# Moving the quantise parts on VectorE from ahead of the factors to ahead of the accumulation

## What is computed

```python
def _L0_attn_ref(hidden_states, w_q, w_k, w_v, w_o):
    q, k, v = ((hidden_states @ w).reshape(B, S, H, Dh) for w in (w_q, w_k, w_v))
    scores = einsum('bqhd,bkhd->bhqk', q, k) * scaling + mask
    attn = softmax(scores, axis=-1)
    return einsum('bhqk,bkhd->bqhd', attn, v).reshape(B, S, H * Dh) @ w_o

def fp4_quant_dequant(x):                     # blocks of 16 along the last dim
    scale = max(max(abs(xb)) / 6.0, 1e-12)
    idx = searchsorted(_MID, abs(xb / scale))
    return _GRID[idx] * sign(xb) * scale

def fp4_linear(x, w):
    return einsum('bsk,nk->bsn', fp4_quant_dequant(x), fp4_quant_dequant(w))
```

## Time and profile before

| | us |
|---|---|
| median of 3 runs | 483.98 |
| lowest to highest | 483.85 to 485.07 |
| the profiled execution | 483.85 |
| its span (first to last instruction) | 482.0 |

### The profile page before, as it was taken

One profiled execution on the slowest core, in us unless ns is written; L12 is line 12 of the kernel. 1 busy time (PEld: TensorE's weight loads), 2 busy tenths in 40 slices (PEclk: granted clock), 3 DMA queues, 4 the chain that ended last, 5 costly groups with the idle time before them and its releaser, 6 DMA issues.

```text
span 482.0 us, 17248 instructions
## 1 busy us (share of the span) xinstructions
PE 442.8 (92%) x6418; PEld 347.0 (72%) x6418; DVE 404.4 (84%) x1368; ACT 331.6 (69%) x972; POOL 298.1 (62%) x501
## 2 busy tenths in 40 slices
PE   0899989999999999999999999999977879989995
PEld 0677777878887888878888778887643746558674
DVE  5887857898889899889798688987999999898674
ACT  3477757767877877867877776875644587986433
POOL 4234548677667758757757676738588896572212
PEclk9999999999999999999999999999999999999999
DMA  7278682355345335335455653543000000000002
GB/s 218 109 214 247 170 258 51 71 109 112 66 88 118 72 72 116 71 74 110 82 120 137 126 110 78 105 90 69 1 1 0 1 1 0 2 1 2 1 0 88
DMA packets 136099, 40.54 MB, mean 84 GB/s; under 512 B 104976, under 2 KB 131024, under 8 KB 136016
## 3 DMA queue, kind: packets, MB, share of 16 engines
q1 hardware_dynamic: 135440, 38.38, 34.5%
q10 hardware_dynamic: 576, 1.05, 0.8%
HBM read 29.44 MB, written 9.96 MB: 82 GB/s over the span
## 4 chain that ended last, share of the span: by engine, by line
PE 63%; POOL 11%; DVE 7%; DMA 6%; SPq 6%; ACT 4%; issue 3%; DVEq 0%; POOLq 0%; ACTq 0%
PE psum L411 10%; PE psum L453 10%; PE psum L473 6%; PE psum L1175 5%; PE psum L487 5%; PE psum L499 5%; PE psum L484 4%; PE psum L392 4%; DMA w_rows_dram<-st 3%; PE psum L1170 3%; POOL area L1843 2%; PE psum L394 2%; PE psum L393 2%; SPq L285 2%; DMA pband<-_attn_hidden_states_dram 2%
## 5 line engine op out<-in xcount | busy, mean ns | idle before, releaser
L936 POOL TENSOR_SCALAR pband<-pband,fac 128x192 f32<-128x192 f32 x256 | 104.4, 430 | 89.1 <-DVE fac L752 89.0
L556 ACT ACTIVATE pband<-pband,st 128x192 f32<-128x192 f32 x256 | 113.2, 448 | 0.1
L700 DVE CUSTOM_DVE_ANT_0 pband<-psum,band_mask 128x192 f32<-128x192 f32 x256 | 76.1, 353 | 1.0 <-PE psum L411 0.8
L411 PE MATMUL psum<-keys,q_class 64*64 64x192 f32 (+2 forms) x1536 | 66.4, 275 | 0.0
L453 PEld LDWEIGHTS psum<-ident,pband 128*128 128x128 f32 x384 | 45.3, 141 | 21.4 <-issue 13.5
L411 PEld LDWEIGHTS psum<-keys,q_class 64*64 64x64 f32 x1536 | 57.5, 133 | 2.9 <-issue 2.0
L453 PE MATMUL psum<-ident,pband 128*128 128x128 f32 x384 | 53.1, 274 | 2.4 <-DVE pt L761 2.4
L556 ACT ACTIVATION_READ_ACCUMULATOR pband<-pband,st 128x1 f32 x256 | 49.4, 193 | 0.0
L918 POOL COPY keys<-k_rows 128x512 f32<-128x512 f32 x32 | 36.3, 1136 | 18.7 <-issue 10.2
L761 DVE COPY pt<-psum 128x512 f32<-128x512 f32 x64 | 43.7, 684 | 3.8 <-PE psum L453 3.6
L926 POOL COPY q_class<-q_rows 128x512 f32<-128x512 f32 x32 | 36.4, 1136 | 11.2 <-ACT q_rows L596 11.2
(11 more groups left out here) (219 smaller groups left out, 1091.7 us busy)
## 6 DMA issues: line engine op xcount, KB each, us to landing
v_rows_dram<-arena SPq DMA_DIRECT2D x32, 256.0 KB, 3.4
v_both<-v_rows_dram SPq DMA_DIRECT2D x32, 256.0 KB, 3.7
v_seg<-v_rows_dram SPq DMA_DIRECT2D x64, 128.0 KB, 3.6
v_side<-v_rows_dram SPq DMA_DIRECT2D x96, 64.0 KB, 2.6
w_rows_dram<-st SPq DMA_DIRECT2D x64, 8.0 KB, 2.9
st<-w_rows_dram SPq DMA_DIRECT2D x64, 8.0 KB, 2.4
arena<-_attn_hidden_states_dram SPq DMA_DIRECT2D x4, 256.0 KB, 4.0
out_dram<-x SPq DMA_DIRECT2D x4, 256.0 KB, 2.8
```

The costliest lines, as they stand in the source:

```text
L411: return pe.matmul(bank[2 * r + head][rows, at:at + y.shape[1]], x, y, start=True, stop=True, skip_group_check=True)
L556: act.activation(x, x, ACT.Exp, bias=mine[:, head:head + 1], scale=-1.0, accum_out=mine[:, 2 + head:3 + head]).then_inc(s_exp, 1)
L700: dve.tensor_tensor_reduce(pband[:, G % P_SLOTS, c, head, :], bank[2 * r + head][:, at:at + BAND], band_mask[:, (0, 1, 1, 2)[w], SEG * (1 ...
L936: pool.tensor_scalar(x, x, fac[:, F % 2, 1, c, head:head + 1], 1.0, ALU.mult, ALU.mult).then_inc(s_scaled, 1)
```

## The change

The call of quantise is moved within DVE's loop over steps: it stood between even_turned(t-5, 0) and factors(t-4), and now stands directly ahead of accumulate(t-6). Its condition and arguments are the same, so each part still runs in the same step number. No other engine's code changes.

```diff
             for t in range(FIRST_STEP, DRAIN):
                 differences(t - 4)
                 even_turned(t - 5, 0)
-
-                if QUANT_STEP <= t < QUANT_STEP + 15:
-                    quantise((t - QUANT_STEP) // 5, (t - QUANT_STEP) % 5)
                 factors(t - 4)
                 band_max(t - 2, 0)
                 seg_max(t - 2, 0)
@@
                     dve.memset(raw[P - R:P, 0:2, 2 * P:FT], 0.0)
                     dve.memset(raw[:, 2, FF:FT], 0.0).then_inc(s_zero, 1)
+                if QUANT_STEP <= t < QUANT_STEP + 15:
+                    quantise((t - QUANT_STEP) // 5, (t - QUANT_STEP) % 5)
                 accumulate(t - 6)
```

## The result

The changed kernel takes 489.18 us (median of 5, 487.32 to 489.67) where the kernel before takes 483.98 (median of 5, 483.69 to 485.07): 5.2 us more by the medians. The ratio is 1.0088, 95% interval 1.0068 to 1.0107, which is 4.3 us. Timed again on another chip the ratio was 1.0101 (1.0072 to 1.0129). The sign was forecast; the size, +2.0 with an upper end of 488.0, was not.

A forecast was written before the change was run, and what follows sets the result against it. PE was taken to bound the kernel, with DVE's delays costing only beyond the room ahead of L773. Port waits of 0.68 + 0.14 + 0.61 + 0.61 = 2.04 us on the 483.98 median gave 486.0 us, range 483.7 to 488.0.

The forecast's parts named there:

- PE is the bound, and its two step lengths: Steps 12 to 26: PE sets the pace, 8.79 or 9.26 us per step, whichever part DVE runs.
- The room ahead of L773: Between L722 and L773, DVE can take 1.35 us more in a short step, 1.82 in a long one, at no price.
- Counting one gate only: L773 freeing the bank for L392 is counted; L731, L735 and copy L761 behind it bind at about the same lateness.
- Off the old place, gain 0: Ahead of factors: removing the parts gains 0; POOL's wait for fac costs nothing and fac hardly comes sooner.
- DVE's idle time before L722 stays: Before the sums L722: the move does not buy off DVE's idle time, since ACT's exponentials end it.
- The one that waits gets the next turn: DVE and POOL alternate by whole instructions on shared ports; a part waits only for what is left of L945, at most 1.06.
- part 0 waits at its scalar steps: Part 0's 24-wide scalar operations wait for POOL too; without that, step 17's term is 0, the forecast some 0.7 lower.
- The terms: Per-step excess over the room ahead of L773: 0.68 us in step 17, 0.14 in 15, 0.61 each in 20 and 25.
- the reason given there: Step 12, part 0: fac comes 1.21 us sooner, no part ahead of it yet, so L945 is over: 0.
- Rival 3: The gate is met in nearly every step, delays passing to the next fac: 4 to 5 us, 488 to 489; chance 0.07.
- Rivals 1 and 2: 1: parts miss L945, 484.0 to 484.7 us (0.36); 2: step 21's PE gap vanishes, 483.5 us (over 0.5 faster: 0.05).
- What would show it: Signs expected in the changed kernel's trace: late L773, longer parts, L945 sometimes 1.5 us, outputs late in steps 15, 17, 20, 25 alone.

## Why the prediction was right or wrong

**PE is the bound, and its two step lengths: right** of the kernel before. The changed kernel shows them, within 0.04 us, in steps 12, 18, 23 and 26 alone. From step 13 on DVE's round has become as long as PE's step or longer, which the prediction didn't work out for any step. It looked at the part's distance to one gate, never at the length of DVE's whole round with waits in it: 9.3 to 9.9 us against PE's 9.03 on average.

**The room ahead of L773: right,** 1.35 us in a short and 1.82 in a long step, within 0.1: in step 20 L392 starts 0.06 us after L773's end. That makes the real room 1.43 and 1.90. Counting one gate only was right too: in the stretch PE never waited for the copy L761.

**Off the old place, gain 0: right** in the time, but POOL's wait for fac did not stay as it was: it grew from 41.2 to 46.9 us.

**"DVE's idle time before L722 stays": wrong.** This is a step that failed. The idle time was the slack that had kept the two engines apart. With a wait of 1.4 us in each of parts 1 to 4 it is used up, to less than 0.1 us, in steps 13 to 26 except 17, which has 0.26 (11.4 us over the run, from 21.2). From then on each late part makes the next L722 late.

**"The one that waits gets the next turn": wrong, the first step that failed.** It rested on one place, step 8. In steps 13 to 26 the first operation of parts 1, 3 and 4 waited for the running copy and for the scaling behind it, 1.8 to 2.0 us in all instead of 0.55, and L845 of part 2 1.76 instead of 0.35. The prediction's bound was what is left of L945, at most 1.06 us, and up to 0.3 more for a start that meets L918; the wait is 1.4. That part 0 waits at its scalar steps was right: L837, one input and a scalar, waits as L1805 of the earlier trace rows does: 0.73 us in step 17 and 1.02 in step 22. The Trainium skill's rule on this (SBUF — State Buffer, SBUF: two separate sides), that the other engine fully blocks for a whole instruction, agrees with that: the 24-element operation takes 0.18 us alone, and in both steps it ends 0.04 us behind the scaling.

**The terms.** Against the forecast, in us of the step's excess:

| step, part | forecast | measured |
|---|---|---|
| 12, part 0 | 0 | 0.01 |
| 13, 16, 18, 21, 23, 26, parts 1 and 4 | 0 | 0.31, 0.31 and the gap, 0.03, 0.48, 0, 0.04 |
| 14, 19, 24, part 2 | 0 | 0.44, 0.22, 0.71 |
| 17, 22, part 0 | 0.68, 0 | 0.34, 0.23 |
| 15, part 3 | 0.14 | 0.48 |
| 20, 25, part 3 | 0.61 each | 1.12, 1.07 |

The two largest are where they were forecast and nearly twice the size. But 2.8 us (and the gap) fall to steps with no term at all, since in a locked round every part has its wait. Step 12 cost nothing for the reason given there, yet it began the chain: with 1.21 us ahead of L773 the fac of step 13 came later, and L842 of step 13 met both POOL operations (139.96, 1.83 us).

**The rivals.** Rival 3 named what happened, its mechanism, its deciding point (the scaling over 0.60 us after L722 in most steps: 0.84 to 1.14 in fourteen of fifteen) and its price, 488 to 489. Given 0.07, it had one argument against it, that a wait of L945 in one step moves it in the next. In steps 12 to 26 the scaling never waited (1.03 to 1.09 us throughout); it moved together with L722, and from step 13 on every part met it. That the price came out is in part luck: it was near the 5.0 us of every part meeting a whole L945, at most 1.06 us each, where the waits were of 1.4. The rival could have been worked out from the trace of before: the scaling stands 5.6 to 5.7 us behind fac there too, and L722, without ACT's hold (steps 9 and 28), 4.6, which puts the scaling 1.1 us behind L722 in every step in which the idle time is used up., with 0.94, show such a step. Rivals 1 and 2 fell: the steps 13 to 17 all lost time, and a gap without a releaser was there as well, in step 16 (0.52), where it had been in step 21. Both places are fixed ones in PE's own sequence, so the place of a gap does not go with DVE's order.

**What would show it.** L773 1.1 to 2.6 us after L722: up to 3.10 in step 20. L945 sometimes at 1.5: no, the scaling kept 1.05, since it was never the one to wait; this line alone would have told the two readings of step 8 apart. Outputs late in steps 15, 17, 20 and 25 alone: no, in seven more steps by 0.2 us or more. "Wrong would be a loss in steps with parts 1 or 4": there was one in steps 13, 16 and 21.

**No better version** came of it. In this stretch the kernel before has no wait of PE for DVE at all and 0.5 us of gap. There is nothing here for a place of the parts to win; the kernel with parts 1 and 4 moved alone is level with it.

## What to carry to other kernels

When two engines share ports and both start their rounds from the same event, work out the whole round of the faster one with the waits in it and compare it with the bound's step, before you compare a moved piece with the room at one gate. Idle time of an engine off the critical path is what keeps such pairs from locking; a cost worked out for each step apart holds only as long as some of it is left. And one place in a trace that shows who goes first isn't a rule: search for the second.

## What the runs showed of the hardware

- A DVE operation with two SBUF inputs that comes up while POOL runs a 512-element copy, with a 512-element product next in POOL's queue, nearly always waits for both (59 of 60 cases, nine of them L845 with its one input): 1.9 us instead of 0.55 in the locked steps. With POOL held back after the copy it is 0.94.
- Beside POOL's 192-element scalings, with one more of them next, the same operation waits for nothing that shows (0.55), and POOL pays, 2.00 us for 1.63. With the 512-element product next it waited for that too (1.77).
- The wait stands in the record as duration, not as idle time. Growing means of a group, with the count unchanged, are the sign.
- In step 8 the order of turns is the other one in all fifteen profiles, for an operation that elsewhere waits for both; so it is once in step 16 (0.90 us). Open.
- Whole runs of one kernel spread over 481.8 to 489.2 us between executions and chips; the stretch between two output products within a profile was repeated to 0.3, 1.0 and 1.4 us (137.7 and 138.0, 141.4 and 140.4, 138.3 and 139.7).
- PE's gaps in the scores without a releaser came to 0.2 to 3.0 us in the stretch, in front of the same three matmuls in every kernel. Their length differs between executions of one kernel (2.2 and 3.0 us with the parts behind L773). Their cause wasn't tried.
